# Second attention layer: scores from one matrix per head and the shared normalised tokens, instead of projected queries and keys

## The reference

```python
xn = _layernorm(x, gamma_media, beta_media)      # context, 77 rows
ln = _layernorm(latents, gamma_lat, beta_lat)    # tokens, 512 rows
q = ln @ Wq + bq
kv = jnp.concatenate([xn, ln], axis=1) @ Wkv + bkv
k, v = jnp.split(kv, 2, axis=-1)
q, k, v = (to_heads(q), to_heads(k), to_heads(v))
q = q * DH ** (-0.5)
sim = jnp.einsum('bhid,bhjd->bhij', q, k)
attn = jax.nn.softmax(sim, axis=-1)
out = jnp.einsum('bhij,bhjd->bhid', attn, v)
out = out.transpose(0, 2, 1, 3).reshape(b, -1, INNER)
return out @ Wo + bo
```

## Time and profile before

| | us |
|---|---|
| median of three runs | 1545.33 |
| the profiled execution | 1546.16 |
| its span in the trace | 1544.4 |
| attention of the second layer, first pair | 162 to 379 |
| the same, second pair | 924 to 1141 |
| before the loop over pairs | 0 to 19.4 |

### The profile page before, as it was taken

One profiled execution on the slowest core, in us unless ns is written; L12 is line 12 of the kernel. 1 busy time (PEld: TensorE's weight loads), 2 busy tenths in 40 slices (PEclk: granted clock), 3 DMA queues, 4 the chain that ended last, 5 costly groups with the idle time before them and its releaser, 6 DMA issues.

```text
span 1544.4 us, 26110 instructions
## 1 busy us (share of the span) xinstructions
PE 1411.3 (91%) x8820; PEld 1130.1 (73%) x8820; DVE 817.1 (53%) x2046; ACT 763.8 (49%) x1652; POOL 124.3 (8%) x115
## 2 busy tenths in 40 slices
PE   5988999999999987899979889999999998888999
PEld 3785567777898765679948746677779887556798
DVE  5793544554434747743357735445534457476532
ACT  4752445555543454554447325455555434545453
POOL 1042000000000002000011410000000100020000
PEclk9999999999999999999989999999999999999999
DMA  5002000000002000000000020000000020000000
GB/s 198 1 2 110 0 1 1 1 1 1 1 1 82 29 1 1 5 1 15 1 17 1 1 110 1 0 1 1 1 1 1 1 110 1 1 1 1 1 8 8
DMA packets 4038, 27.88 MB, mean 18 GB/s; under 512 B 1055, under 2 KB 1345, under 8 KB 2881
## 3 DMA queue, kind: packets, MB, share of 16 engines
q1 hardware_dynamic: 3040, 21.50, 3.6%
q10 hardware_dynamic: 864, 4.64, 0.8%
HBM read 25.09 MB, written 1.05 MB: 17 GB/s over the span
## 4 chain that ended last, share of the span: by engine, by line
issue 68%; PE 19%; DVE 7%; POOL 3%; ACT 2%; DMA 0%; DVEq 0%; SPq 0%; POOLq 0%; ACTq 0%
PE psum L658 17%; DVE nmax L1341 2%; POOL rs L1199 1%; PE psum L680 1%; DVE rsum L1350 1%; POOL arenaD L1212 1%; ACT arenaB L988 1%; POOL x L1224 1%; DVE arenaA L1561 1%; ACT arenaA L988 1%; DVE xn L1296 1%; DVE psum L1337 0%; DMA mask<-in_mask_dram 0%; DVE x L1373 0%; ACT probs L988 0%
## 5 line engine op out<-in xcount | busy, mean ns | idle before, releaser
L658 PEld LDWEIGHTS psum<-moe,arenaA 128*128 128x128 f32 x2048 | 239.1, 194 | 8.1 <-issue 1.9
L658 PE MATMUL psum<-moe,arenaA 128*128 128x128 f32 x2048 | 241.4, 277 | 2.2 <-DVE gt L1443 1.4
L988 ACT ACTIVATE arenaB<-psum 128x512 f32<-128x512 f32 x448 | 170.1, 432 | 147.0 <-PE psum L680 146.9
L988 ACT ACTIVATE probs<-psum,nmax 128x589 f32<-128x589 f32 (+1 forms) x256 | 125.9, 555 | 162.8 <-DVE nmax L1417 157.2
L988 ACT ACTIVATE arenaA<-psum,vec 128x512 f32<-128x512 f32 (+1 forms) x208 | 125.5, 615 | 157.2 <-PE psum L658 156.8
L658 PE MATMUL psum<-arenaD,arenaB 128*128 128x128 f32 (+2 forms) x1440 | 188.5, 279 | 10.7 <-ACT arenaB L988 9.8
L1417 DVE TENSOR_REDUCE nmax<-psum 128x1 f32<-128x589 f32 x128 | 98.7, 771 | 174.8 <-PE psum L658 174.6
L658 PEld LDWEIGHTS psum<-arenaD,arenaB 128*128 128x128 f32 (+1 forms) x1440 | 173.4, 193 | 22.1 <-issue 10.9
L1398 DVE SCALAR_TENSOR_TENSOR x<-psum,gt,x 128x128 f32<-128x128 f32 x256 | 72.1, 345 | 213.8 <-PE psum L658 213.8
L658 PE MATMUL psum<-parts 128*128 128x512 f32 x672 | 166.9, 398 | 0.0
L680 PE MATMUL psum<-w_first,probs 128*128 128x128 f32 (+2 forms) x1120 | 159.4, 273 | 3.2 <-ACT arenaA L988 3.1
(11 more groups left out here) (198 smaller groups left out, 1853.6 us busy)
## 6 DMA issues: line engine op xcount, KB each, us to landing
moe<-in_w_moe_dram SPq DMA_DIRECT2D x4, 4096.0 KB, 13.3
moe<-in_w_folds_dram SPq DMA_DIRECT2D x2, 1024.0 KB, 9.0
w_l<-in_w_l_dram ACTq DMA_DIRECT2D x1, 1372.0 KB, 12.3
x<-in_x_dram SPq DMA_DIRECT2D x4, 256.0 KB, 3.9
w_l<-in_w_l_dram ACTq DMA_DIRECT2D x1, 1024.0 KB, 9.5
out_dram<-x SPq DMA_DIRECT2D x4, 256.0 KB, 2.1
w_rest<-in_w_rest_dram ACTq DMA_DIRECT2D x1, 768.0 KB, 7.1
w_first<-in_w_first_dram ACTq DMA_DIRECT2D x1, 596.0 KB, 5.4
```

Source lines behind the costliest of these rows:

```text
L658: return nc.tensor.matmul(out, lhsT, rhs, start=start, stop=stop, skip_group_check=shared)
L988: return nc.scalar.activation(out, in_, func, **kw)
```

## The change

For each head the product of query and key weights, times the scale, is made once ahead of the loop (`cross1`, in `fold`). A query projection uses that product, and the scores are taken against the normalised tokens `xnT` and context `mnT` themselves, which now lie in one tile. `keys1` and `media_keys1` are gone. The query bias becomes a vector per head, added to the projected queries (`turns1`, part 0). The key bias would add the same to a whole column's worth of keys of one query: it becomes one number per row and head (`shift1`), made by the new step `shifts1` (four matmuls of 8 columns per sequence). Everything is negated: one DVE instruction adds the shift to the negated scores, writes them to SBUF and takes the row's minimum, and frees the slot; ACT takes the exponential from SBUF, in place, with scale -1. The third load of 1 MB (`w_folds2`) is on SP's queue, the load `l1` on ACT's queue is gone. `schedule()` puts `shifts1(0)` where the first `keys1` stood and `shifts1(1)` at step 22.

```diff
@@ schedule()
-                        3: (lambda: do("media_keys1", 0, 0, gen()), lambda: do("media_keys1", 0, 1, gen())),
-                        4: (lambda: do("media_keys1", 1, 0, gen()), lambda: do("media_keys1", 1, 1, gen())),
...
+    do("shifts1", 0, gen())
     do("queries1", 0, 0, gen())
-    do("keys1", 0, 0, gen())
...
+        if k == half // 4 + 14:
+            do("shifts1", 1, spare(k))
...
-        if k % NT == 1 and k + NT - 1 < n:
-            do("keys1", *units[k + NT - 1][:2], spare(k))
@@ SP
-            for i in range(2):
+            for i in range(3):
                 sp.dma_start(moe[:, 2048 * i:2048 * i + 2048], dram[f"w_folds{i}"]).then_inc(loaded_folds[i].sem, 16)
@@ TensorE, fold()
                 for h in range(H1):
-                    last = mm(slot(G0, 128), bv1[:, h, :], wo1[:, h, :], start=h == 0, stop=h == H1 - 1)
+                    mm(slot(G0, 128), bv1[:, h, :], wo1[:, h, :], start=h == 0, stop=h == H1 - 1)
+                pe.wait_ge(loaded_folds[2].sem, 16)
+                pe.wait_ge(loaded_small.sem, 16 * NSMALL)
+                for h in range(H1):
+                    mm(slot(G0, 1, at=128 + h), wk1[:, h, :], V("bq1", h))
+                    mm(slot(G0, 1, at=136 + h), wq1[:, h, :], V("bk1", h))
+                    last = mm(slot(G0, 1, at=144 + h), bq1[:, h, :], V("bk1", h))
+                last.then_inc(folded.sem, 1)
+                for h in range(H1):
+                    if h == 4:
+                        last.then_inc(folded.sem, 1)
+                        pe.wait_ge(fold_kept.sem, 1)
+                    last = mm(slot(G1, 128, at=128 * h) if h < 4 else psum[:, 128 * h - 512:128 * h - 384], wq1[:, h, :], wk1[:, h, :])
                 last.then_inc(folded.sem, 1)
...
+            def shifts1(s, i):
+                read(i, "norm", 2, s)
+                take(i)
+                for t in range(NT):
+                    last = mm(slot(i, H1, at=H1 * t), xnT[:, s, t * 128:(t + 1) * 128], turns1[:, 1, :])
+                last.then_inc(*filled[i].mark("shift", s))
...
-                mm(slot(i, L), W["wq1"][:, 128 * h:128 * h + 128], xnT[:, s, :]).then_inc(*filled[i].mark("q1", s, h))
+                mm(slot(i, L), cross1[:, h, :], xnT[:, s, :]).then_inc(*filled[i].mark("q1", s, h))
...
-                mm(slot(i, L), q, kh[:, h % 2, :])
-                mm(slot(i, KEYS, at=512), q, kmedia[:, s, h, :]).then_inc(*filled[i].mark("s1", s, h, t))
+                mm(slot(i, L), q, xnT[:, s, :])
+                mm(slot(i, KEYS, at=512), q, mnT[:, s, :]).then_inc(*filled[i].mark("s1", s, h, t))
@@ ACT
-                f(qh[:, h % 2, :], slot(i, L), ACT.Identity, scale=float(128 ** -0.5), bias=scaled[:, 2 + h:3 + h])\
-                    .then_inc(*free[i].mark("q1", s, h))
+                f(qh[:, h % 2, :], slot(i, L), ACT.Identity, bias=turns1[:, 0, h:h + 1]).then_inc(*free[i].mark("q1", s, h))
...
-                act.wait_ge(*nmax_ready.at(s, h, t))
-                f(row_probs[k % 4], slot(i, 589), ACT.Exp, bias=nmax[:, k % 4, 0:1], accum_out=rsum[:, k % 4, 0, 0:1])\
-                    .then_inc(*free[i].mark("s1", s, h, t))
+                act.wait_ge(*least_ready.at(s, h, t))
+                f(row_probs[k % 4], row_probs[k % 4], ACT.Exp, scale=-1.0, bias=nmax[:, k % 4, 0:1], accum_out=rsum[:, k % 4, 0, 0:1])\
+                    .then_inc(*exp1_ready.mark(s, h, t))
...
-            load("rest0", "l1", "l2", "l3")
+            load("rest0", "l2", "l3")
...
-            act.wait_ge(fold_kept.sem, 6)
+            act.wait_ge(folded.sem, 5)
+            f(cross1[:, 0:4, :].rearrange("p h c -> p (h c)"), slot(G1), ACT.Copy, scale=-float(128 ** -0.5)).then_inc(fold_kept.sem, 1)
+            act.wait_ge(folded.sem, 6)
+            f(cross1[:, 4:8, :].rearrange("p h c -> p (h c)"), psum[:, 0:512], ACT.Copy, scale=-float(128 ** -0.5)).then_inc(fold_kept.sem, 1)
+            act.wait_ge(fold_kept.sem, 8)
@@ POOL, clear_keys0
+                if s == 1:
+                    pool.wait_ge(folded.sem, 6)
@@ DVE
+            def shifts1(s, i):
+                dve.wait_ge(*filled[i].at("shift", s))
+                v.tensor_tensor(shift1[:, s, :, :], slot(i, NT * H1).rearrange("p (t h) -> p t h", t=NT),
+                                turns1[:, 2, :].unsqueeze(1).broadcast_to([128, NT, H1]), ALU.add).then_inc(*free[i].mark("shift", s))
+                dve.wait_ge(*free[i].at("shift", s))
 
             def softmax1(s, h, t, k, i):
                 dve.wait_ge(*filled[i].at("s1", s, h, t))
-                v.tensor_reduce(nmax[:, k % 4, 0:1], slot(i, 589), AX, ALU.max, negate=True).then_inc(*nmax_ready.mark(s, h, t))
+                dve.sem_inc(held_dve.sem, 1)
+                v.tensor_tensor_reduce(row_probs[k % 4], slot(i, 589), shift1[:, s, t, h:h + 1].broadcast_to([128, 589]),
+                                       1.0, 3.0e38, ALU.add, ALU.min, nmax[:, k % 4, 0:1]).then_inc(*free[i].mark("s1", s, h, t))
+                dve.wait_ge(*free[i].at("s1", s, h, t))
+                dve.sem_inc(*least_ready.mark(s, h, t))
                 if k:
                     scale_row(k - 1)
...
+            v.tensor_copy(bq1[:, :, :], vec[:, a:a + 8].unsqueeze(2).broadcast_to([128, 8, 128])).then_inc(spread.sem, 1)
...
             v.tensor_tensor(b2, slot(G0, 128), b2, ALU.add).then_inc(spread.sem, 1)
-            dve.wait_ge(spread.sem, 2)
+            v.tensor_scalar(turns1[:, :, :].rearrange("p n h -> p (n h)"), slot(G0, 24, at=128), -float(128 ** -0.5), None, ALU.mult)\
+                .then_inc(spread.sem, 1)
+            dve.wait_ge(spread.sem, 3)
```

More of the change, by code:

```diff
@@ L46 @@
 W_L3 = [("wq3", 128), ("wk3", 128), ("wv3", 128), ("wo3", 128), ("gate3", 8)]
-W_GROUPS = [("first", W_FIRST), ("second", W_SECOND), ("rest0", W_REST0), ("l1", W_L1), ("l2", W_L2), ("l3", W_L3)]
+W_GROUPS = [("first", W_FIRST), ("second", W_SECOND), ("rest0", W_REST0), ("l2", W_L2), ("l3", W_L3)]
 VECS = [("qw", 1), ("qb", 1), ("kw", 1), ("kb", 1), ("b1_0", 4), ("gm", 1), ("bm", 1), ("gl", 1), ("bl", 1),
@@ L466, in program @@
         v0 = [a.rearrange("p (g c e) -> p g c e", g=2, c=CHUNKS) for a in (arenaD[:, 0:1280], moe[:, 5376:6656])]
-        wv0, wu0, wv1, wo1, bv1 = [moe[:, 1024 * i:1024 * i + 1024].rearrange("p (m c) -> p m c", m=8) for i in range(5)]
+        wv0, wu0, wv1, wo1, wq1, wk1, bv1, bq1 = [moe[:, 1024 * i:1024 * i + 1024].rearrange("p (m c) -> p m c", m=8)
+                                                  for i in range(8)]
         W["wv1"] = mix1[:, :, :].rearrange("p h e -> p (h e)")
@@ L507, in program @@
         loaded_small = signal("loaded_small")
-        loaded_folds = [signal(f"loaded_folds{i}") for i in range(2)]
+        loaded_folds = [signal(f"loaded_folds{i}") for i in range(3)]
         folded = signal("folded")
@@ L537, in program @@
         probs1_ready = signal("probs1_ready")
-        nmax_ready = signal("nmax_ready")
+        least_ready = signal("least_ready")
+        exp1_ready = signal("exp1_ready")
         kbd0_clear = signal("kbd0_clear")
@@ L836, in values1, with queries1, scores1 @@
                 mm(slot(i, 512, p), lhs, W["wv1"][:, 512 * h:512 * h + 512]).then_inc(*filled[i].mark("v1", s, c, h))
-            def media_keys1(s, h, i):
-                need(pe, "wk1")
+            def shifts1(s, i):
[4 more added lines that the diff above has]
+                last.then_inc(*filled[i].mark("shift", s))
+            def queries1(s, h, i):
+                take(i)
+                mm(slot(i, L), cross1[:, h, :], xnT[:, s, :]).then_inc(*filled[i].mark("q1", s, h))
+            def scores1(s, h, t, i):
+                read(i, "q1", s, h)
                 read(i, "media", s)
                 take(i)
-                for m in range(4):
-                    c = 128 * (4 * h + m)
-                    last = mm(slot(i, KEYS, at=KEYS * m), W["wk1"][:, c:c + 128], mnT[:, s, :])
-                last.then_inc(*filled[i].mark("km1", s, h))
-            def queries1(s, h, i):
-                take(i)
-                mm(slot(i, L), W["wq1"][:, 128 * h:128 * h + 128], xnT[:, s, :]).then_inc(*filled[i].mark("q1", s, h))
-            def keys1(s, h, i):
-                take(i)
-                mm(slot(i, L), W["wk1"][:, 128 * h:128 * h + 128], xnT[:, s, :]).then_inc(*filled[i].mark("k1", s, h))
-            def scores1(s, h, t, i):
-                read(i, "q1", s, h)
-                read(i, "k1", s, h)
-                take(i)
                 q = qh[:, h % 2, t * 128:(t + 1) * 128]
-                mm(slot(i, L), q, kh[:, h % 2, :])
-                mm(slot(i, KEYS, at=512), q, kmedia[:, s, h, :]).then_inc(*filled[i].mark("s1", s, h, t))
+                mm(slot(i, L), q, xnT[:, s, :])
+                mm(slot(i, KEYS, at=512), q, mnT[:, s, :]).then_inc(*filled[i].mark("s1", s, h, t))
             def turn_probs1(s, h, t, k, r, i):
@@ L1102, in values1 @@
                 f(v1[s][0:p, c, 512 * h:512 * h + 512], slot(i, 512, p), ACT.Copy).then_inc(*free[i].mark("v1", s, c, h))
```

(15 more changed lines are left out.)

33 lines of the change are left out of this document (15 added, 18 removed).

## The result

The changed kernel takes 1534.5 us (median of five runs, 1532.07 to 1537.35) against 1545.33 before: a ratio of 0.9933, interval 0.9919 to 0.9946. The forecast was 1530 in a range of 1519 to 1546. So it is faster, by 10.8 us, where 15 were forecast. The profiled execution took 1535.79 us with a span of 1533.6.

What follows compares the result with a forecast made beforehand. TensorE's order bounds the second layer's attention, DVE the first's, with a row chain nearly as long beside TensorE. From 1546.16 us: -27.3 + 1.8 + 0.8 + 5.1 - 0.6 + 5.0 = -15.2, so 1531.0, or 1530 against the median; range 1519 to 1546.

Steps and rivals of the forecast that it cites:

- Key projections: Second layer's attention loops: 15 key projections per pair removed from TensorE at 0.91 us each, a gain of 27.3 us.
- The beginning of each loop: First mixing waits for ACT's copies anyway, so 0.4 us per pair of the gain is lost: +0.8 (0 to 1.8).
- Shift, second sequence: Four 8-column matmuls on TensorE, eight passes at 0.11, 0.88 us; over two pairs +1.8 us.
- Row chain: Scores to copies, each unit: +0.15 us, 0.07 covered, 0.08 excess, paid twice per head: 5.1 us (0 to 18).
- the cover: Row chain in the loop: it reaches TensorE 0.07 us early, so only additions beyond 0.07 become a stall.
- 64 paying units: Count for the row chain's excess: two of a head's four steps pay, over 32 heads.
- The accumulator, priced at 0.08: Row chain, DVE's fused instruction: +0.08 us for writing its accumulator, nearest to an ACT read lasting 0.19.
- DVE's instruction at half rate: Rival: every unit's reduction lasts 1.4 us instead of 0.77, costing 43 us instead of 5.1, giving 1568; chance 0.09.
- Start: Fold ahead of the loops: 48 one-column passes at 0.11 delay DVE's signal; net +5.0 us (3.5 to 8).
- the cover of 0.8: Start: product matmuls and ACT's copies were to stay hidden before the transposes, with about 0.8 us to spare.
- Late third load: Rival at the start: ACT's large rows win the engines, TensorE waits to 23 or so, +4, giving 1534; chance 0.11.
- Longer stall: Rival in the row chain: accumulator costs 0.25 or so, excess 0.25, 16 us in all, giving 1541; chance 0.13.

Runs made afterwards that it cites:

- e_plain: Changed kernel with the fused instruction undone: DVE takes the minimum in PSUM, ACT reads PSUM and frees the slot, shift made but not added; 1525.3 us.
- v_noshift: `e_plain` without making the shift, 8 one-column matmuls instead of 24, placed behind the products, folded bias signalled to DVE ahead of both; 1513.18 us.
- e_more: Changed kernel plus a DVE copy of the 128x1 minimum and a wait for it ahead of the signal to ACT; 1546.3 us.
- e_direct: Changed kernel without DVE's wait for its own result: the fused instruction releases ACT itself, and the exponential frees the slot; 1529.5 us.
- e_signal_early: Changed kernel with the bias fold signalling DVE before the one-column passes, whose results go to another bank and are moved by ACT; 1534.7 us.
- v_narrow24: `v_noshift` plus 16 more matmuls of one column (32 passes, results unused); 1519.6 us.
- v_wide24: `v_noshift` plus 16 more matmuls of 128 columns (32 passes, results unused); 1517.2 us.
- e_plain_held: `e_plain` with the separate DVE signal left between DVE's wait for the scores and its instruction; 1524.2 us.
- b_held: Kernel before the change with a separate DVE signal between its wait and the row maximum, nothing else; 1548.9 us.

## Why the prediction held, and where it did not

The time lies in the range and moved as forecast, and the two main mechanisms, the order of TensorE in the loop and the row chain beside it, are the ones that the runs show. That the total is only 4.5 off is in part luck: the row chain cost 5.8 more than forecast, and the key projections, with shift and loop beginnings, gave 2.4 more.

**Key projections.** The step was right and somewhat too small. `e_plain` has everything but the longer chain, and its loop is 13.55 us per pair shorter, shift included: -27.1 for both against -27.3 + 1.8 + 0.8 = -24.7. The plain head pays 0.86 (12.76 to 11.90). Heads with other work on the path pay more, 1.24 in the fourth (16.94 to 15.70): there the key projection stood in front of late work of DVE or ACT and its price was more than its place (in the fifth head of the kernel before it waits 0.27 for DVE's copy of the values). I had taken all 15 at the plain price.

**The beginning of each loop.** I took back 0.4 us per pair. The first two heads are 1.23 and 0.45 shorter in `e_plain`, together 1.68 of the 1.82 of two key projections, so 0.1 was lost and not 0.4.

**Shift, second sequence.** Right: +0.84 per pair by `v_noshift`, 0.88 forecast.

**Row chain.** The mechanism was right and the size off by a factor of two: 10.9 instead of 5.1. In the plain heads two errors cancelled. The addition is 0.21 instead of 0.15 and the cover 0.10 instead of 0.07, so the excess is 0.11 where 0.08 was forecast, and the eighth head pays 0.17 against 0.16. That agreement is partly luck: two stalls of 0.11 would be 0.22, and what the trace has is three units longer by 0.05 to 0.06, while heads 11 and 14 pay 0.11. In `e_more` the eighth head does pay twice. What went wrong is the factor of 64 paying units, which took every head for a plain one. Where TensorE waited already for a copy that ACT makes behind the exponential, nothing covers the chain (0.25 in heads 4 to 6). Where DVE runs without a gap, its own wait and the late reciprocal make each unit of DVE longer, and that goes to TensorE. The term priced neither.

Part by part, the addition came from elsewhere than forecast. The accumulator, priced at 0.08, costs nothing behind the instruction: in `e_direct` the second gap is 0.81 with the read in it, as before. DVE's own wait and signal cost 0.06 there (0.87 against 0.81), for 0.05 forecast. The signal between the wait for the scores and the instruction had no price in the forecast and costs 0.11, the fused form another 0.04. The exponential's source in SBUF lasts longer (0.79 against 0.75) and delays nothing, since the copies start 0.79 behind its start in both kernels, where 0.025 was forecast.

**DVE's instruction at half rate.** Refuted. The group of all fused instructions, whole span (count, busy us, mean ns, idle before):

```profile
L1425 DVE CUSTOM_DVE_ANT_0 probs<-psum,shift 128x589 f32<-128x589 f32 x128 | 98.7, 771 | 166.5 <-PE psum L659 164.4 <-DVE gt L1471 0.9 <-DVE gt L1486 0.4
L1425 DVE DVE_READ_ACCUMULATOR2_ANT nmax<- 128x1 f32 x128 | 10.6, 83 | 0.0
```

It streams as fast as the maximum did, 771 ns with one source in PSUM. The Trainium skill (Vector Engine (DVE) Microarchitecture Reference, Points that are easy to get wrong) names the halved rate only for two sources in SBUF that are not bf16. This row agrees with it; the case of two such sources no run here shows.

**Start.** The sum was nearly right (+5.69 against +5.0), its reason wrong, and so the agreement is luck. The prediction had DVE's signal set the start and TensorE's fold end 0.8 us ahead of it. `e_signal_early` shows that an earlier signal gains nothing: the fold ends as late by itself. What I missed is the clock. I had said that without the idle gap it would stay at 2.4 GHz, but it fell under the one-column passes, 48 of which took 6.63 us instead of 5.3, and the 16 product passes took 3.76 us; at full clock 16 such passes took 2.05 in `v_narrow24`. So the cover of 0.8 was gone.

**Late third load.** Not in this kernel: TensorE doesn't wait for it. In the profiled run of `e_more`, whose start is the same code, it did for 0.99 us. There the clock fell earlier as well (0.79 from 19 to 22 us, 0.50 from 22 to 34), the 48 one-column passes took 9.14 us instead of 6.63, and the first row maximum came at +10.5 instead of +5.7. The start differs by that much between executions.

**Longer stall.** The rival at 1541 put the term at 16 us, about as far above the measured 10.9 as the forecast's 5.1 was below. Its reason, an accumulator of 0.25 in each chain, is refuted by `e_direct`.

## What to carry to other kernels

When a second chain is nearly as long as the bounding engine's order, price an addition to it by the units that are not regular as well: those in which something behind the same engine is waited for already, and those in which the engine that got the new instruction has no gap. Count the added instruction's length on its own engine, waits for its own result included; here that wait cost more than the rest of the addition. Before moving a bias through a kernel, ask whether it changes the result: here the kernel without it, and with the row chain and the fold's start changed too, was 21 us faster still, twice what the change brought. Reordering the fold alone gained nothing (1534.7 and 1535.4), and with 48 passes in the order of the fastest kernel the start was as late as ever (76.73). And price matmuls of one column by their passes: eight of them, 16 passes, took 1.84 us, nearly as long as 16 passes of 128 columns (2.05).

## What the hardware showed unexpectedly

- TensorE's granted clock fell to 1.2 GHz while it was busy all the time, under 48 one-column passes (kernel after: 0.66 and 0.50 in the windows from 22 and 25.5 us). After 16 of them (`v_noshift`), or 16 among 32 of 128 columns (`v_wide24`), it was 1.00 up to 29.5 us.
- A signal by a separate instruction between a wait and the next DVE instruction delays that instruction by 0.11 us (0.38 to 0.49), in both kernels in which it was added alone (`e_plain_held`, `b_held`).
- A 128x1 copy with a wait for its own result adds 0.19 us to a chain, of which the copy is 0.15.
- DVE's wait for its own result adds 0.06 us to the chain (0.81 to 0.87), yet 3.19 us to a loop of 64 units (`e_direct` against the kernel after).
- A fused addition with row minimum over 589 elements takes 771 ns and its accumulator read 83 ns.
